# Scan step of a two-layer Mamba-2 kernel: dt in four passes, totals on VectorE, one carry product per sequence, output tile 0 grouped, and the step's work in a new order

## What is computed

```python
zxbcdt = u @ in_w.T                            # z 512, x 512, B 64, C 64, dt 8 columns
dt = softplus(dt + dt_bias); dA = exp(dt * A)  # one value per head and token
xBC = silu(conv4(xBC) + conv_b)                # causal, 4 taps
state = dA_t * state + (dt_t * x_t)[..., None] * B_t    # scan over the tokens
y_t = einsum('bhpn,bn->bhp', state, C_t)
y = (y + D * xh) * silu(z)
y = y * rsqrt(mean(y * y) + EPS) * rms_w
h = y @ out_w.T + h
```

## Time and profile before

| | |
|---|---|
| median of 3 runs | 2084.46 us (2078.38 to 2094.24) |
| profiled execution | 2084.11 us, its span 2081.9 us |
| busy over the span | PE 1865.5 (90%), PEld 1385.4 (67%), DVE 1577.4 (76%), ACT 1260.9 (61%), POOL 943.5 (45%) |
| granted TensorE clock | mean 0.966 of full speed |

### The profile page before, as it was taken

How to read it: one execution, slowest core, us unless ns; L and a number is a source line. 1 busy time by engine, 2 the same in 40 slices (tenths; PEclk the granted TensorE clock), 3 DMA queues, 4 the chain that set the end, 5 groups by cost and what they waited for, 6 DMA issues and landing times. The chain is left out here.

```text
span 2081.9 us, 37447 instructions
## 1 busy us (share of the span) xinstructions
PE 1865.5 (90%) x12544; PEld 1385.4 (67%) x12544; DVE 1577.4 (76%) x3503; ACT 1260.9 (61%) x2237; POOL 943.5 (45%) x840
## 2 busy tenths in 40 slices
PE   5899999999999999999999999999856888888887
PEld 4566666666676677776766677766645676666665
DVE  4777888787788867877778777787547878888885
ACT  3666667666666757776677677677403444444443
POOL 2566566666656555554555565455501111111110
PEclk9999999999999999999999999999967999999999
DMA  3011111111111111111121111110031111011100
GB/s 134 21 37 36 37 53 47 40 35 35 35 35 52 49 36 37 41 37 37 35 64 36 40 35 35 35 51 30 16 101 41 61 58 33 30 60 60 60 21 20
DMA packets 87250, 91.68 MB, mean 44 GB/s; under 512 B 4928, under 2 KB 82448, under 8 KB 87184
## 3 DMA queue, kind: packets, MB, share of 16 engines
q1 hardware_dynamic: 79360, 79.46, 11.8%
q10 hardware_dynamic: 7824, 11.37, 2.2%
HBM read 57.26 MB, written 25.17 MB: 40 GB/s over the span
## 5 line engine op out<-in xcount | busy, mean ns | idle before, releaser
L852 POOL TENSOR_TENSOR L_xc<-L_xpad,L_vec 128x512 f32<-128x512 f32 x160 | 166.1, 1038 | 320.2 <-ACT L_xpad L650 320.2
L1595 POOL TENSOR_TENSOR M_rstd<-M_var,M_power 128x4 f32<-128x4 f32 x64 | 71.3, 1115 | 461.4 <-DVE M_var L156 461.4
L374 PE MATMUL L_front<-L_uhi,L_whi 128*128 128x512 f32 x576 | 250.5, 435 | 10.3 <-DVE L_xc L1065 7.0
L1077 DVE TENSOR_TENSOR L_m<-L_dbank,L_gm 128x512 f32<-128x512 f32 x256 | 172.9, 686 | 101.5 <-ACT L_dbank L690 101.5
L1553 ACT ACTIVATE M_nrm<-M_lin,M_shift,M_rstd 128x256 f32<-128x256 f32 x192 | 92.7, 563 | 242.5 <-POOL M_shift L1603 242.5
L844 POOL TENSOR_TENSOR L_yg<-L_yg,L_sz 128x512 f32<-128x512 f32 x128 | 165.3, 1291 | 162.0 <-DVE L_yg L1092 160.8
L522 PE MATMUL L_mix<-L_wo,L_yg 128*128 128x256 f32 x1024 | 235.0, 383 | 2.6 <-POOL L_yg L844 2.6
L374 PE MATMUL L_front<-L_uhi,L_wlo 128*128 128x512 f32 x576 | 229.8, 399 | 0.0
L374 PE MATMUL L_front<-L_ulo,L_whi 128*128 128x512 f32 x576 | 229.7, 399 | 0.0
L522 PEld LDWEIGHTS L_mix<-L_wo,L_yg 128*128 128x128 f32 x1024 | 191.8, 192 | 27.5 <-POOL L_yg L844 2.8
L650 ACT ACTIVATE L_xpad<-L_front,L_pbias 128x512 f32<-128x512 f32 x160 | 110.1, 689 | 154.2 <-PE L_front L374 154.2
(11 more groups left out here) (176 smaller groups left out, 4797.6 us busy)
## 6 DMA issues: line engine op xcount, KB each, us to landing
h<-L_hres SPq DMA_DIRECT2D x32, 512.0 KB, 3.0
L_hin<-in_x SPq DMA_DIRECT2D x16, 512.0 KB, 4.6
L_hres<-in_x SPq DMA_DIRECT2D x16, 512.0 KB, 3.8
L_cc<-L_xc ACTq DMA_DIRECT2D x64, 128.0 KB, 2.3
L_hin<-h SPq DMA_DIRECT2D x16, 512.0 KB, 4.6
L_hres<-h SPq DMA_DIRECT2D x16, 512.0 KB, 3.8
M_hin<-h SPq DMA_DIRECT2D x16, 512.0 KB, 3.8
M_xin<-in_x SPq DMA_DIRECT2D x16, 512.0 KB, 4.6
```

What stands on the lines that cost most here:

```text
L374: last = nc.tensor.matmul(to[:, :], ww[:, kd, tile * P:(tile + 1) * P], a[:, kd, :], start=i == 0, stop=i == len(passes) - 1)
L852: nc.gpsimd.tensor_tensor(xc[p][:, q, :].rearrange("p (b i) -> p b i", b=NB), xpad[:, q, :, 0:P], vector(layer, "conv_w", q * TAPS, 1).uns ...
L1077: nc.vector.tensor_tensor(m[:, b, 4 * half:4 * half + 4, :], dbank[half][:, :].rearrange("p (h i) -> p h i", i=P), gm[:, b, :].unsqueeze(1 ...
```

## The change

`project_dt` keeps the rounded low part of the dt weights beside the high part (16 columns of `whi`), so that one pass gives high and low products in 16 rows. Four passes stand where six did, and DVE adds the two halves after the transpose (`dtlow`, then `dtraw`). `sum_da` makes two products in place of three; DVE adds the total (`total`). `carry` is one product per sequence in place of two; its moving operand `dpair` is a new GpSimd operation, `pair_operands` (1024 bf16 elements). `outputs(n, 0)` is grouped as the other tiles: eight `within` products, then eight `carried` ones. All four engines' `step` gets a new order. The diff cut to its core; in the hunks of `step` only the lines of the new order that the diff adds stand (its removed lines are in the listing above), and a row that is only "..." marks a cut.

```diff
+                passes = [(2 * NH, 0, uhi), (NH, 0, ulo), (NH, 1, ulo), (2 * NH, 1, uhi)]
+                for i, (wide, kd, a) in enumerate(passes):
+                    last = nc.tensor.matmul(front[0][0:wide, :], whi[:, kd, NPROJ - NH:NPROJ - NH + wide], a[:, kd, :],
+                                            start=i == 0, stop=i == len(passes) - 1, skip_group_check=True)
                 last.then_inc(proj, 1)
...
-                for i, matrix in enumerate((tri, suffix, ones)):
+                for i, matrix in enumerate((tri, suffix)):
...
                 if b == 0:
+                    pe.wait_ge(dpair_done, n + 1)
                     pe.wait_ge(dtx_done, NB * n + 4)
                 elif b == 1:
                     pe.wait_ge(bt_done, n + 1)
                 else:
                     pe.wait_ge(cs_done, NB * n + b - 1)
                 rows = slice(ROWS * (b % 2), ROWS * (b % 2) + ROWS)
-                moving = dmov[rows, b // 2, :, :].rearrange("r (t o) i -> r t o i", o=2)
-                for odd in range(2):
-                    last = nc.tensor.matmul(mix[b % 2][:, :], sel[rows, odd, :], moving[:, :, odd, :], start=odd == 0, stop=odd == 1)
-                last.then_inc(ec_ready, 1)
+                nc.tensor.matmul(mix[b % 2][:, :], sel[rows, :], dpair[rows, b // 2, :, :], start=True, stop=True).then_inc(ec_ready, 1)
...
             def outputs(n, p, t):
                 if t == 0:
+                    pe.wait_ge(cs_done, NB * n + NB)
                     pe.wait_ge(m_done, 8 * n + 8)
                     wait(pe, state_done, 2 * (n - 1))
                     if isinstance(n, int) and n < GROUPS:
                         pe.wait_ge(cleared, 1)
                 wait(pe, y_skip, T * n + t - 1)
...
+                for b in range(NB):
+                    within(n, t, b)
+                for b in range(NB):
+                    last = carried(n, p, t, b)
                 last.then_inc(y_ready, 1)
```

PE's step:

```diff
                 more, more2 = follows(n, 1), follows(n, 2)
+                turn_x(n, p, 0)
                 if more:
                     project_conv(n + 1, 0)
                     turn_dt(n + 1)
+                decays(n, 4)
                 if follows_any(n):
                     result(n - 1, layer_of(n, layer, -1), 1)
                 if more:
                     project_conv(n + 1, 1)
                 turn_x(n, p, 1)
+                turn_x(n, p, 2)
                 decays(n, 5)
+                turn_x(n, p, 3)
                 decays(n, 6)
                 if more:
                     project_conv(n + 1, 2)
+                carry(n, 0)
+                decays(n, 7)
                 turn_b(n, p)
                 carry(n, 1)
+                carry(n, 2)
                 if more:
                     project_conv(n + 1, 3)
                 carry(n, 3)
+                new_state(n, 0)
+                if more:
+                    project_conv(n + 1, 4)
+                new_state(n, 1)
                 outputs(n, p, 0)
                 outputs(n, p, 1)
+                outputs(n, p, 2)
+                if more:
                     sum_da(n + 1)
                 outputs(n, p, 3)
                 if more:
                     turn_cum(n + 1)
@@ -589,18 +586,18 @@
                     project_z(n + 1, 1)
                     project_z(n + 1, 2)
                     project_z(n + 1, 3)
                     decays(n + 1, 0)
                     decays(n + 1, 1)
+                    scores(n + 1, 1 - p)
                 if more2:
                     turn_u(n + 2, p)
                 square_sums(n)
                 if starts_layer(n + 2):
                     fold_bias(layer_of(n, layer, 2))
+                result(n, layer, 0)
+                if more:
+                    decays(n + 1, 2)
+                    decays(n + 1, 3)
                 if more2:
```

GpSimd:

```diff
+            def pair_operands(n):
+
+                pool.wait_ge(dops, 2 * n + 2)
+                wait(pool, ec_ready, NB * n)
+                nc.gpsimd.tensor_tensor(dpair[:, :, :, :], dmovT[:, :, :].unsqueeze(2).broadcast_to([P, 2, T, P]),
+                                        pairs[:, :, :].unsqueeze(1).broadcast_to([P, 2, T, P]), ALU.mult).then_inc(dpair_done, 1)
...
+                to_end(n, p, 0)
                 if more:
                     first_tap(n + 1, layer1, 1 - p, 0)
                     first_tap(n + 1, layer1, 1 - p, 1)
                 decay_state(n, p)
+                if more:
+                    first_tap(n + 1, layer1, 1 - p, 2)
                 to_end(n, p, 1)
                 to_end(n, p, 2)
+                to_end(n, p, 3)
+                if more:
+                    first_tap(n + 1, layer1, 1 - p, 3)
+                    first_tap(n + 1, layer1, 1 - p, 4)
+                if more2:
+                    layer_norm(n + 2)
+                gate(n, 0)
+                gate(n, 1)
+                if next_layer == 0:
+                    norm_residual(n + 1, c + p, 1 - p)
+                gate(n, 2)
+                add_squares(n, 1)
+                gate(n, 3)
+                add_squares(n, 2)
+                add_squares(n, 3)
+                if more:
+                    second_operands(n + 1)
+                rsqrt(rrms, ssq, ss_done, n, rr_done)
                 if twice:
                     model_norm(n + 2, p)
                 if more:
+                    pair_operands(n + 1)
```

VectorE, the new sums, and its step:

```diff
+                turned = front[0][:, :].rearrange("p (b h) -> p b h", b=NB)
+                nc.vector.tensor_tensor(dtlow[:, :, :], turned[:, :, NH:2 * NH], dtb[:, layer, :].unsqueeze(1).broadcast_to([P, NB, NH]),
+                                        ALU.add).then_inc(dt_low, 1)
+                dve.wait_ge(dt_low, n + 1)
+                nc.vector.tensor_tensor(dtraw[:, :, :], turned[:, :, 0:NH], dtlow[:, :, :], ALU.add).then_inc(dt_biased, 1)
...
                 part(0, cum)
+                nc.vector.tensor_tensor(total[:, :, :], cum, sums[:, 1, :, :], ALU.add).then_inc(total_done, 1)
                 dve.wait_ge(split, 5 * n + 1)
                 rest(rest1, cum, 0)
...
+                weigh(n, 3)
+                scale_x(n, p, 0)
                 if more:
                     set_halo(n + 1, 1 - p)
+                    bias_dt(n + 1, layer1)
+                weigh(n, 4)
+                if more:
+                    convolve(n + 1, layer1, 1 - p, 0, 0)
+                    convolve(n + 1, layer1, 1 - p, 0, 1)
+                if follows_any(n):
+                    finish(n - 1, layer_of(n, layer, -1), None, 1 - p, 1)
+                if more:
+                    convolve(n + 1, layer1, 1 - p, 0, 2)
+                scale_x(n, p, 1)
+                scale_x(n, p, 2)
+                if more:
+                    convolve(n + 1, layer1, 1 - p, 1, 0)
+                scale_x(n, p, 3)
+                weigh(n, 5)
+                if more:
+                    convolve(n + 1, layer1, 1 - p, 1, 1)
+                    convolve(n + 1, layer1, 1 - p, 1, 2)
+                scale_c(n, 0)
+                if more:
+                    convolve(n + 1, layer1, 1 - p, 2, 0)
+                scale_c(n, 1)
+                scale_c(n, 2)
+                if more:
+                    convolve(n + 1, layer1, 1 - p, 2, 1)
+                    convolve(n + 1, layer1, 1 - p, 2, 2)
+                scale_c(n, 3)
+                weigh(n, 6)
+                if more:
+                    convolve(n + 1, layer1, 1 - p, 3, 0)
+                weigh(n, 7)
                 if more2:
                     layer_moments(n + 2, layer2, chunk2, p)
                 if more:
                     convolve(n + 1, layer1, 1 - p, 3, 1)
                     convolve(n + 1, layer1, 1 - p, 3, 2)
+                skip(n, layer, p, 0)
+                if more:
                     convolve(n + 1, layer1, 1 - p, 4, 0)
                 skip(n, layer, p, 1)
                 if more:
                     convolve(n + 1, layer1, 1 - p, 4, 1)
+                    finish_dt(n + 1, layer1, 1 - p)
+                    convolve(n + 1, layer1, 1 - p, 4, 2)
                 skip(n, layer, p, 2)
                 if more:
+                    split_sums(n + 1)
                     decay_operands(n + 1)
+                add_state(n, p, 0)
                 skip(n, layer, p, 3)
                 if more:
                     first_operands(n + 1)
                 add_state(n, p, 1)
                 if ends_sequence(n) and more2:
                     clear_halo(n, p)
+                mean_square(n)
                 if more:
                     mask_scores(n + 1)
                     weigh(n + 1, 0)
                 if starts_layer(n + 2):
                     fold_rows(layer2)
                 if more2:
                     rest_u(n + 2, 0)
+                if more:
+                    weigh(n + 1, 1)
+                if more2:
                     rest_u(n + 2, 1)
+                finish(n, layer, c, p, 0)
                 if more:
                     weigh(n + 1, 2)
```

(5 more changed lines are left out.)

180 lines of the change are left out of this document (51 added, 129 removed).

## The result

| | before | after |
|---|---|---|
| median us | 2085.36 (2078.38 to 2094.24, 4 runs) | 2166.06 (2158.46 to 2172.85, 4 runs) |
| ratio of the times | | 1.038, 95% interval 1.033 to 1.044 |
| profiled execution, span us | 2081.9 | 2171.1 |
| PE / DVE / POOL busy us | 1865.5 / 1577.4 / 943.5 | 1884.5 / 1629.5 / 1013.4 |
| matmuls | 12544 | 12288 |

The account below looks back on a forecast made before the run. It took PE to bound the kernel before and a PE-DVE ring with chained GpSimd stalls after: 15.5 x 2.85 + 15.5 x 0.85 = 57 us on 2084.1 gives 2141 us (chance 0.38), own range 2110 to 2160, full range 2045 to 2190.

Parts of the forecast that it names:

- What bounds the kernel now: Whole step before the change: PE bounds, busy 43.2 of 45.65 us in layer 0 and 43.1 of 45.07 in layer 1.
- The 0.95 us for tile 0: Output tile 0 on PE: grouping it like tile 1 cuts 2.94 us to 1.99, booked as 0.95 us saved per step.
- The ring: New order's fixed chain through PE and DVE, (a) plus (b): without stalls 43.4 us in layer 0, 43.1 in layer 1.
- (a): PE's part of the ring, from turn_cum of the next item to turn_x(1): 22.7 us.
- (b): DVE's part of the ring, from scale_x(1) to the last operation of split_sums: 20.6 us in layer 0, 20.4 in layer 1.
- The stalls: GpSimd instructions hold DVE's short operations in finish_dt and split_sums: 5.1 us a step in layer 0, 2.8 in layer 1.
- the walk: Layer 0 timeline from the end of weigh(7), operation by operation: split_sums ends at 14.8 us, against 9.75 free of stalls.
- Rival 2: PE's waits lower its clock in the z tiles: up to 1.7 us a step, up to 53 us more, 2194; chance 0.22.
- Rivals 1 and 3: Rival 1 has its own line; 3: PE's removed work is gained in full, 85 us less, 1999 us, chance 0.02.
- Rival 1: Stalls in finish_dt and split_sums don't chain: few, 2062 us, chance 0.18; none, 2019 us, chance 0.12.
- the 0.85 us of a layer 1 step: Layer 1 step: ring plus 2.8 us of stalls makes 45.9 us, 0.85 more than before.
- 15.5 steps of each layer: Whole scan: the 31 steps counted as 15.5 at 2.85 us and 15.5 at 0.85 us more, 57 us in all.

Follow-up runs that it names:

- e6: The change's work reductions in the old order (as e1), but tile 0 ungrouped as before and pair_operands ahead of the last rsqrt; 2078.6 us, ratio 1.000.
- e8: The kernel before with one edit, output tile 0 grouped; 2140.3 us, ratio 1.027.
- e3: The change, with GpSimd made to wait behind gate(n, 1) until VectorE has finished split_sums; 2138.0 us, ratio 1.024.
- e5: e3 with norm_residual moved from behind the held place to behind first_tap(3); 2068.4 us, ratio 0.994.
- e9: e5 with GpSimd held back one instruction sooner, ahead of gate(n, 1); 2065.1 us, ratio 0.991.
- e4: The change, with six unused products more ahead of sum_da and four more ahead of turn_cum on TensorE; 2148.4 us, ratio 1.030.
- e10: The kernel before's work in the new order of all engines, with GpSimd held back and norm_residual early as in e5; 2107.1 us, ratio 1.012.
- e1: The change's work reductions with all engines in the order of the kernel before, pair_operands last on GpSimd; 2148.5 us, ratio 1.030.
- e7: e1 with five unused products more on TensorE ahead of the grouped output tile 0; 2104.8 us, ratio 1.011.

## Why the prediction was right or wrong

**Sign and range** were right (slower, 2045 to 2190). The time, 2141, was 25 us short, and 2166 lies above the forecast's own range of 2110 to 2160; the full range holds it because it was widened for the clock. In the profiled executions the 14 steady steps of layer 0 brought 34.7 us for 39.9 forecast, the 15 of layer 1 30.7 for 12.8, and the rest of the span 23.9 for about 5.

**What bounds the kernel now: wrong.** The prediction said that TensorE bounds it, from 43.2 busy of 45.65 us. e6 took 1.1 us of this busy time away and gained 0.15, and e8 lost 0.84 us by a wait in a place where the prediction had booked a gain. The reader would have seen it in the earlier trace rows: tile 0 took 2.94 us there, and VectorE did `scale_c` meanwhile. That was cover, not cost. The last two `scale_c` of that step run beside the first half of the tile:

```profile
359.92 1.29 DVE L1087 TENSOR_TENSOR L_cs<-L_mix,L_cc 128x512 f32<-128x512 f32 x2 [0.54 <-ACT L_mix L699]
```

The sentence "PE isn't waiting for them", of the short VectorE operations before the change, doesn't hold either: `skip(1)` starts at 370.72, behind `split_sums` and one `convolve` without a gap, and it is the `skip` for which tile 3 waits 0.79 us in the earlier trace rows. The path from `sum_da` to tile 3 thus ran through VectorE in the kernel before too. The price of the removed work was also too high: 1.8 us were booked for dt, carry and `sum_da` together, and TensorE's busy time fell by 1.1 in e6.

**The 0.95 us for tile 0: wrong in the old order.** A tile that is done in parts behind each of its producers is longer but ends sooner. The new order hides this, with `new_state`, `project_conv(4)` and `new_state` between the last `scale_c` and tile 0: at 376.51 in the change it starts without a wait.

**The ring: right.** (a) + (b) without stalls was 43.4 and 43.1 us. e3 in layer 1 measured 43.7 with one held operation of 0.63 us left, thus 43.1; e5 in layer 0 measured 45.1 with 0.63 in `finish_dt` and 1.24 in `layer_moments`, thus 43.2. Below 43.4 it didn't fall in layer 1 (e9), since TensorE's tail bounds next.

**The stalls: right in kind, 0.75 us too long in layer 0.** Forecast were 48.5 and 45.9; measured 47.75 and 45.76. From the end of `weigh(7)` (376.29) the walk had the held rows end at 7.2, 9.3, 11.4, 12.8 and 14.2; they ended at 7.15, 9.0, 11.0, 12.25 and 13.5, five of five in the order forecast, behind the same GpSimd rows. The 0.7 us is a sum of small excesses: the walk let each GpSimd instruction lose time to the short operation that goes in ahead of it, and they took no longer than they do alone (1.90, 1.89, 1.32, 1.26). One detail was wrong: `total` doesn't wait for the first cast, went in together with it and took 0.18 us, so the fourth and fifth held rows are the two operations behind it. In layer 1 the rows were 0.82, 1.16 and 1.30 us, for 0.7, 0.8 and 1.3 lost.

The Trainium skill (SBUF — State Buffer, "Who interferes with whom") gave the lock, held for a whole instruction. The runs agree: each held row ends within 0.1 us of a GpSimd row's end, and in e9 all rows of `finish_dt` and `split_sums` are at 0.18 to 0.22 us. The chain is in the rows as well. A held operation ends with the GpSimd instruction that held it, the next one needs its result and starts some 0.03 us later, and by then GpSimd's next instruction has its row: GpSimd at 383.35 ahead of VectorE's 383.47, and at 388.45 ahead of 388.57.

**Rival 2, the clock, given 0.22, came true beside the forecast and not instead of it.** Its 1.7 us in the z tiles measured 1.55, but in layer 1, three steps of four, and not in layer 0, where the prediction had the longer waits: there the stretch fell in tile 3, beside VectorE. It is worth 18 us by e4. Adding it to 2141 gives 2159.

**Rivals 1 and 3** fell: the stalls chain, and no gain of PE's work appears. (Rival 1's layer 1 step with two held operations should read 44.4, 43.1 + 1.3, and not 44.6.) Rival 1's price without any stall, 2019 us for 43.4 and 43.1, was near for layer 1 alone and too low for the whole: e9 takes 2065 us, with 43.4 us in layer 1 and 44.8 in layer 0, where `norm_residual` now holds `layer_moments` for 1.2 us.

**What failed in the sum** is two of its terms. One is the 0.85 us of a layer 1 step, which left out the clock: these steps grew by 2.05 us on average. The other is "15.5 steps of each layer", which takes the step over the change of layers and the two ends as steady steps. 29 steady steps brought 65.4 us, where the forecast had 14 x 2.85 + 15 x 0.85 = 52.7, and the rest of the span another 23.9. In the step over the layers `project_dt` waits for the new layer's weights, which are folded on VectorE, a wait that has no row before:

```profile
804.21 0.61 PE L364 MATMUL L_front<-L_uhi,L_whi 128*16 128x512 f32 x1 [5.43 <-DVE L_whi L958]
```

The same wait of 5.43 us stays in e5, and its step over the layers is 59.9 us (61.2 in e9) against 55.5. e10, with the old work in the new order, waits 5.15 us there and has 61.2 us; e1, with the new work in the old order, has no such wait and 55.0. So it is the new order that brings it. Behind the last `turn_cum` the scan ends 4.8 us later, and the MLP, the same code, takes 566.8 instead of 558.9 us, with a granted clock of 0.91 in a 100 us window where it was 0.97. In e7 it took 554.7 us. Why its clock differs from kernel to kernel was not tried and stays open.

**Costs put at nothing.** `pair_operands` was free in the new order: beside it (354.04 to 356.16) no short operation runs. In e1's order it held one for 0.86 us. `keep_b`'s wait was 0.56 us for 0.7 forecast, and lay beside VectorE.
